# Step sizes of a selective scan: x products one batch ahead, the last batch turned in four banks, the scan's first block beside it

## What is computed

```python
u2 = silu(conv(u) + conv_b)                  # 4 batches x 512 tokens x 512 channels
dbl = u2 @ W_x                               # 48 columns: 16 dt_low, 16 B, 16 C
dt = softplus(dt_low @ W_dt + b_dt)          # step sizes
A = -exp(A_log)
def step(h, inp):                            # 16 states per channel
    dt_t, B_t, C_t, u_t = inp
    dA = exp(dt_t[:, :, None] * A)
    h = dA * h + (dt_t * u_t)[:, :, None] * B_t[:, None, :]
    return h, einsum('bdn,bn->bd', h, C_t)
y = scan(step) + u2 * D
y = y * silu(z)
out = y @ W_out
```

## Time and profile before

| | |
|---|---|
| time before, median of 3 runs | 1596.59 us (1590.95 to 1600.13) |
| the profiled execution | 1599.52 us |
| its span in the profile | 1597.7 us |
| TensorE busy | 1447.3 us (91%) |
| VectorE busy | 1068.1 us (67%) |
| ScalarE busy | 853.1 us (53%) |
| GpSimd busy | 477.2 us (30%) |
| the stage: last z products end, first scan starts | 249.3 us, 333.0 us |

### The profile page before, as it was taken

One profiled execution on the slowest core, in us unless ns is written; L12 is line 12 of the kernel. 1 busy time (PEld: TensorE's weight loads), 2 busy tenths in 40 slices (PEclk: granted clock), 3 DMA queues, 4 the chain that ended last, 5 costly groups with the idle time before them and its releaser, 6 DMA issues.

```text
span 1597.7 us, 20215 instructions
## 1 busy us (share of the span) xinstructions
PE 1447.3 (91%) x7408; PEld 988.6 (62%) x7420; DVE 1068.1 (67%) x1218; ACT 853.1 (53%) x1509; POOL 477.2 (30%) x140
## 2 busy tenths in 40 slices
PE   5898797689899999897999889999989999999997
PEld 3566343278797988743443433333358888888886
DVE  6996495669889898865443457777564565565655
ACT  3433456489989897641432358777733433333332
POOL 0999120059888897600211420000000000000000
PEclk7899999789999999978999989999999999999999
DMA  7110010502233111502012222344000000000000
GB/s 268 40 43 1 1 53 2 199 27 80 106 99 113 67 54 41 175 1 41 20 40 69 81 80 60 102 135 134 1 0 1 1 14 1 1 14 1 14 1 14
DMA packets 36624, 87.61 MB, mean 55 GB/s; under 512 B 8350, under 2 KB 24948, under 8 KB 32948
## 3 DMA queue, kind: packets, MB, share of 16 engines
q1 hardware_dynamic: 36532, 86.39, 16.3%
HBM read 68.10 MB, written 18.21 MB: 54 GB/s over the span
## 4 chain that ended last, share of the span: by engine, by line
PE 55%; DVE 2%; ACT 2%; issue 2%; DVEq 1%; ACTq 0%
PE ps L1424 12%; PE ps L1433 12%; PE ps L1292 4%; PE ps L1365 4%; PE ps L1159 3%; PE ps L1280 2%; PE ps L1185 2%; PE ps L1121 2%; PE ps L991 1%; PE ps L584 1%; ACT arena L1884 1%; PE ps L1334 1%; PE ps L1043 1%; PE ps L1193 1%; PE ps L1171 1%
## 5 line engine op out<-in xcount | busy, mean ns | idle before, releaser
L2567 POOL TENSOR_TENSOR arena<-arena 128x2048 f32<-128x2048 f32 x63 | 287.3, 4579 | 168.4 <-DVE arena L2107 168.2
L2107 DVE TENSOR_TENSOR_SCAN arena<-arena,ps 128x1024 f32<-128x1024 f32 x128 | 284.2, 2272 | 45.0 <-ACT arena L1727 22.4
L1727 ACT ACTIVATE arena<-arena,mam 128x511 f32<-128x511 f32 x256 | 165.9, 708 | 34.4 <-DVE arena L2107 34.4
L1884 ACT ACTIVATE arena<-ps,rho 128x512 f32<-128x512 f32 x256 | 158.9, 688 | 31.3 <-PE ps L1365 29.9
L2339 DVE TENSOR_REDUCE mxs<-ps 128x1 f32<-128x512 f32 x224 | 141.1, 684 | 44.9 <-PE ps L1280 43.0
L979 PE MATMUL ps<-early,arena 128*128 128x128 f32 x768 | 129.7, 277 | 18.2 <-DVE arena L2107 17.8
L1424 PE MATMUL ps<-early,arena 128*128 128x256 f32 x512 | 127.1, 380 | 2.9 <-DVE mam L2506 1.8
L1913 ACT ACTIVATE arena<-arena 128x256 f32<-128x256 f32 x192 | 85.5, 500 | 81.6 <-DVE arena L2510 50.3
L2547 POOL TENSOR_TENSOR arena<-arena 128x4096 f32<-128x4096 f32 x16 | 115.0, 7189 | 43.4 <-DVE arena L2026 43.4
L1715 ACT ACTIVATE arena<-arena,early 128x512 f32<-128x512 f32 x192 | 123.7, 707 | 0.1
L991 PE MATMUL ps<-early,arena 128*128 128x128 f32 x1024 | 121.5, 272 | 0.9 <-POOL arena L2567 0.7
(11 more groups left out here) (351 smaller groups left out, 2486.8 us busy)
## 6 DMA issues: line engine op xcount, KB each, us to landing
arena<-bc_scratch SPq DMA_DIRECT2D x32, 512.0 KB, 3.7
arena<-in_ffn SPq DMA_DIRECT2D x8, 1024.0 KB, 4.8
batch_scratch<-arena SPq DMA_DIRECT2D x2, 3072.0 KB, 9.1
arena<-batch_scratch SPq DMA_DIRECT2D x6, 1024.0 KB, 6.9
arena<-q_scratch SPq DMA_DIRECT2D x96, 64.0 KB, 2.2
arena<-k_scratch SPq DMA_DIRECT2D x96, 64.0 KB, 2.2
arena<-in_dec_w SPq DMA_DIRECT2D x1, 3855.0 KB, 16.1
arena<-in_cond SPq DMA_DIRECT2D x1, 3739.5 KB, 11.5
```

Source lines behind the costliest of these rows:

```text
L1727: last = act.activation(decay[:, (2 * k + h) % 3, i, 1:S], dt[b % 2][:, m, 1:S], ACT.Exp, scale=a_neg[:, m * NS + n:m * NS + n + 1])
L1884: act.activation(pt[:, j % 4, i], ps[:, 3 + (hg + n) % 3, :], ACT.Exp, scale=rho[:, 0:1]).then_inc(s_pt, 1)
L2107: dve.tensor_tensor_scan(half, view(decay[:, (2 * k + h) % 3], [[1, 2 * S]]), view(ps[:, FEED + 2 * h, :], [[1, 2 * S]]), 0.0, ALU.mult, A ...
L2567: pool.tensor_tensor(state[:, k % SLOTS], state[:, k % SLOTS], view(c_rows[:, j % 2, k % G, :], [[0, M], [1, S]]), ALU.mult).then_inc(s_hc, 1)
```

## The change

- TensorE runs the x products of batch i + 1 between the two halves of the step-size products of batch i; those of the second batch behind both halves of the first; those of the first batch between the last two groups of z products, into bank 0. ScalarE's copy into `dbl` moves accordingly: the first between the last two gates, the others behind the Ln of the first half.
- B's transposes stand between the two halves as before, behind the x products.
- `turn_du` and `turned_du` take the banks as an argument. Batches one to three use 6 and 7 twice, as before. The last uses 6 and 7 and then 4 and 5, with no wait between.
- The D products of the first batch stand ahead of the last `turn_du`; the zero that they read is a column of `one` (two wide now) instead of a place in `decay`.
- ScalarE runs `times_b(0)` ahead of the last batch's two copies of du.
- The wait for the second weight load, and for all gates, moves to where it is needed.

```diff
             for b in range(B):
                 for h in range(2):
                     z_products(b, h)
                     if b + 1 < B:
                         u_products(b + 1, (2 * h, 2 * h + 1))
+                    if b == B - 1 and h == 0:
+                        pe.wait_ge(s_up, B * M + 1)
+                        x_products(0, 0)
...
-            for i, b in enumerate(ORDER):
-                pe.wait_ge(s_u2, (b + 2) * M)
-                pe.wait_ge(s_dbl, i + 1)
-                for m in range(M):
-                    last = pe.matmul(ps[0:48, 4, :], w_x[:, m, :], u2[b][:, m, :],
-                                     start=(m == 0), stop=(m == M - 1))
-                last.then_inc(s_x_mm, 1)
-                pe.wait_ge(s_dbl, i + 2)
...
+            for i, b in enumerate(ORDER):
+                pe.wait_ge(s_dbl, i + 2)
+                dt_products(i, 0)
+                if 0 < i < B - 1:
+                    x_products(i + 1, 4)
+                if i:
+                    pe.wait_ge(s_bt, i)
+                else:
+                    pe.wait_ge(s_sz, 2 * B)
+                for t in range(TILES):
+                    last = pe.transpose(ps[:, 5, t * 64:(t + 1) * 64], dbl[0:64, b * S + t * P:b * S + (t + 1) * P],
+                                        ident[0:64, 0:64])
+                last.then_inc(s_bt_mm, 1)
+                dt_products(i, 1)
+                if i == 0:
+                    x_products(1, 4)
+                else:
+                    turn_du(i - 1, (6, 6))
+            pe.wait_ge(s_dt, 2 * B)
+            d_term(0, range(TILES))
+            pe.wait_ge(s_dbl, B + 1)
+            pe.wait_ge(s_bt, B)
+            turn_du(B - 1, (6, 4))
+            pe.wait_ge(s_duT, 2 * B)
+            pe.wait_ge(s_ends, 1)
...
+            def dbl_out(i, bank):
+                act.wait_ge(s_x_mm, i + 1)
+                act.activation(dbl[0:48, tok(ORDER[i])], ps[0:48, bank, :], ACT.Copy).then_inc(s_dbl, 1)
...
+                    if b == B - 1 and h == 0:
+                        act.wait_ge(s_rows, 1)
+                        dbl_out(0, 0)
...
+                    act.activation(soft_l[:, h], soft_e[:, h], ACT.Ln, bias=one[:, 0:1]).then_inc(s_soft, 1)
+                    if h == 0:
+                        if i < B - 1:
+                            dbl_out(i + 1, 4)
+                        act.wait_ge(s_bt_mm, i + 1)
+                        act.activation(bt[:, b], view(ps[:, 5, :], [[64, TILES], [1, NS]], RANK), ACT.Copy).then_inc(s_bt, 1)
+                if i:
+                    turned_du(i - 1, (6, 6))
+            act.wait_ge(s_ends, 1)
+            act.drain()
+            times_b(0)
+            turned_du(B - 1, (6, 4))
+            act.wait_ge(s_dt, 2 * B)
```

More of the change, by code:

```diff
@@ L226, in program @@
         diag = sb("diag", [P, M, P])
-        one = sb("one", [P, 1])
+        one = sb("one", [P, 2])
         at = 0
@@ L910, in _, with x_products @@
             pe.wait_ge(s_lo_out, B // 2 + 1)
+            def x_products(i, bank):
+                b = ORDER[i]
+                pe.wait_ge(s_u2, (b + 2) * M)
+                pe.wait_ge(s_dbl, i + 1)
+                for m in range(M):
+                    last = pe.matmul(ps[0:48, bank, :], w_x[:, m, :], u2[b][:, m, :],
+                                     start=(m == 0), stop=(m == M - 1))
+                last.then_inc(s_x_mm, 1)
             for b in range(B):
@@ L915, in _, with dt_products, turn_du @@
                         u_products(b + 1, (2 * h, 2 * h + 1))
-            pe.wait_ge(s_sz, 2 * B)
-            pe.wait_ge(s_mam, 32)
-            def turn_du(i):
+                    if b == B - 1 and h == 0:
+                        pe.wait_ge(s_up, B * M + 1)
+                        x_products(0, 0)
+            def dt_products(i, h):
+                if i:
+                    pe.wait_ge(s_dt, 2 * i - 1 + h)
+                for m in (2 * h, 2 * h + 1):
+                    last = pe.matmul(ps[:, m, :], wm["w_dt"][:, m * P:(m + 1) * P], dbl[:, tok(ORDER[i])],
+                                     start=True, stop=True)
+                last.then_inc(s_dt_mm, 1)
+            def turn_du(i, banks):
                 pe.wait_ge(s_du, i + 1)
@@ L923, in turn_du @@
                     if i or r:
-                        pe.wait_ge(s_duT, 2 * i + r)
+                        pe.wait_ge(s_duT, 2 * i + (r if banks[0] == banks[1] else 0))
                     for t in (2 * r, 2 * r + 1):
                         for m in range(M):
-                            last = pe.transpose(ps[:, 6 + t % 2, m * P:(m + 1) * P], du[:, m, t * P:(t + 1) * P], ident)
+                            last = pe.transpose(ps[:, banks[r] + t % 2, m * P:(m + 1) * P], du[:, m, t * P:(t + 1) * P],
+                                                ident)
                     last.then_inc(s_duT_mm, 1)
-            for i, b in enumerate(ORDER):
-                pe.wait_ge(s_u2, (b + 2) * M)
-                pe.wait_ge(s_dbl, i + 1)
-                for m in range(M):
-                    last = pe.matmul(ps[0:48, 4, :], w_x[:, m, :], u2[b][:, m, :],
-                                     start=(m == 0), stop=(m == M - 1))
-                last.then_inc(s_x_mm, 1)
-                pe.wait_ge(s_dbl, i + 2)
[L938 to L959, removed]
+            nought = one[:, 1:2].bitcast(BF16)[:, 0:1]
             def d_term(b, tiles):
@@ L1682, in turned_du @@
                     act.wait_ge(s_duT_mm, 2 * i + r + 1)
[L1683 to L1706, removed]
+                    act.activation(duT[ORDER[i]][:, 2 * r:2 * r + 2, :], ps[:, banks[r]:banks[r] + 2, :],
+                                   ACT.Copy).then_inc(s_duT, 1)
             def times_b(k):
@@ L1733, in turned_back @@
                 act.activation(view(zT[b], [[S, 2], [1, S]]), ps[:, 0:2, :], ACT.Copy).then_inc(s_g01, 1)
+            for i, b in enumerate(ORDER):
+                for h in range(2):
+                    act.wait_ge(s_dt_mm, 2 * i + h + 1)
+                    if i:
+                        act.wait_ge(s_dt, 2 * i - 1 + h)
+                    act.activation(soft_e[:, h], ps[:, 2 * h:2 * h + 2, :], ACT.Abs)
+                    act.drain()
+                    act.activation(soft_e[:, h], soft_e[:, h], ACT.Exp, scale=-1.0)
+                    act.drain()
+                    act.activation(soft_l[:, h], soft_e[:, h], ACT.Ln, bias=one[:, 0:1]).then_inc(s_soft, 1)
[4 more added lines that the diff above has]
+                        act.activation(bt[:, b], view(ps[:, 5, :], [[64, TILES], [1, NS]], RANK), ACT.Copy).then_inc(s_bt, 1)
+                if i:
+                    turned_du(i - 1, (6, 6))
+            act.wait_ge(s_ends, 1)
+            act.drain()
+            times_b(0)
+            turned_du(B - 1, (6, 4))
+            act.wait_ge(s_dt, 2 * B)
             for k in range(B * NS):
-                times_b(k)
+                if k:
+                    times_b(k)
                 if k > NS and k % NS == 4:
@@ L2027, in _ @@
                                   kx_row(t, [[0, H], [1, H]], RECIP), ALU.mult).then_inc(s_att, 1)
-            dve.memset(one[:, :], 1.0)
+            dve.memset(one[:, 0:1], 1.0)
+            dve.memset(one[:, 1:2], 0.0)
             dve.wait_ge(s_h0, B * C)
```

5 lines of the change are left out of this document (3 added, 2 removed).

## The result

The changed kernel takes 1585.45 us (median of 7 runs, 1580.31 to 1590.20), the kernel before beside it 1596.59: a ratio of 0.9944, 95% interval 0.9922 to 0.9967. A second comparison, 12 runs of the changed kernel, gave 0.9957, interval 0.9936 to 0.9978. (The quotients of the medians themselves are 0.9930 and 0.9973.) So the change saves 7 to 9 us, about half a per cent. The profiled execution has a span of 1587.3 us, against 1597.7.

What follows compares the result with a forecast made beforehand. A ring of waits among TensorE, ScalarE and VectorE was taken to bound the stage. Ring 3.4 us, 8.7 with the tail, 6.7 arriving: 1599.52 becomes 1592.8, less 2.9 for the median, 1589.9; range 1581 to 1598.5.

Steps and rivals of the forecast that it cites:

- rival 1: Scan start: ScalarE's lost lead doesn't matter, so the whole 8.7 us gain arrives, 1587.9 us; chance 0.15.
- Entry: First batch's x between the last z groups: first Abs 0.45 us earlier, the table load becoming late.
- First lap: Up to the second batch's second Abs: loses 3.0 us because x stands between the two halves of step sizes.
- Second and third lap: Between later batches' second Abs: 15.6 us where it was 17.8, then 13.2 where it was 17.4.
- Tail: Last dt to first scan: D products ahead of the four-bank turns, scan at 324.3, 8.7 us earlier.
- rival 3: Last turns of du: transposes behind matmuls run at 1.2 GHz, gain 4.8 us, 1591.8; chance 0.07.
- What arrives: Scan's first batch: ScalarE, its lead lost, paces; 6.7 of the 8.7 us goes through to the end.
- (2): TensorE keeps 2.4 GHz over the stage's shorter waits: 16.9 us earlier, about 11 if only some restarts are spared; chance 0.20.
- (4): The stage's ring of waits stays at 1.2 GHz, slower than before: 7.5 us later, 1604.1; chance 0.04.
- (5): The ring isn't shortened, x being late as its copy waits on ScalarE's queue: gain about 1 us, 1595.6; chance 0.10.

Runs made afterwards that it cites:

- experiment 1: Changed kernel with both decays of block 0 ahead of ScalarE's last two du copies; first gate 91.0 us behind the last dt instead of 92.9 to 93.7.
- experiment 6: Changed kernel with the first batch's x products behind z, their copy behind the table load; first gate 159.9 us from the last-but-one z group's start, instead of 162.2 to 162.7.
- experiment 7: Changed kernel with third and fourth batches' x products in TensorE's waits; first gate 155.4 us from the last-but-one z group's start, instead of 162.2 to 162.7.
- experiment 5: Changed kernel with TensorE passes nobody reads in its waits; first gate 154.4 us from the last-but-one z group's start, instead of 162.2 to 162.7.
- experiment 2: Changed kernel with the first batch's D products back behind the last turn of du; first gate 94.4 us behind the last dt instead of 92.9 to 93.7.

## Why the prediction held, and where it missed

The forecast was 1589.9 and a gain of 6.7 us; measured were 1585.45 and, at the first gate, 8.5 to 9.4 us by profiles. The gain is a little above the 5 to 8 which the forecast had given itself, and as a number alone rival 1's 8.7 fits better; but rival 1's mechanism is refuted by experiment 1, and the forecast's is borne out step by step, with one term mis-sized. By its own steps:

- **Entry**: forecast 0.45 us, measured 0.15 (14.4 against 14.5 from S). The table load became late, as said; experiment 6 shows it.
- **First lap**: a loss of 3.0 us at the second Abs of batch two forecast, 3.7 measured in the first profile and 2.5 in the two others. x between the halves at 1.2 GHz is what does it: step sizes 3.75 and x 4.71 us (265.22, 268.90). Experiment 7 takes it out and turns the loss into a small gain.
- **Second and third lap**: this is the term that was mis-sized. Forecast 15.6 and 13.2, measured 14.7 and 12.2 to 13.1. I had put turn and first half of step sizes behind the wait at 2.0 + 3.45 us, since each restart was to bring 5 us of 1.2 GHz. In the second lap they take 4.4 in all three profiles, in two ways: in the first the turn is at full clock and the step sizes aren't (280.29 and 281.22, above); in another the turn is slow and the step sizes are so only in part:

```profile
281.19 1.97 PE L944 MATMUL ps<-early,arena 128*128 128x128 f32 x8 [3.49 <-ACT arena L1706]
282.95 2.71 PE L933 MATMUL ps<-arena,mam 128*128 128x512 f32 x4
```

  At full clock the two take 2.7 (experiment 5), so this restart costs 1.7 us. In the kernel before a restart cost 2.8 and 2.4: the turn 1.97 instead of 1.04, and x 5.46 in one lap and 5.12 in the other instead of 3.63. In the third lap turn and step sizes take 4.4 in the first profile and 5.3 in the two others, so there it is cheaper in the first alone. Why a restart costs less in the new ring, though the wait before it is as long (3.49 us in the second lap, 3.42 and 4.55 before), stays open. The last dt came 1.3 to 1.6 us ahead of the forecast.
- **Tail**: D products at 6.6 us forecast; 6.2 to 7 measured. The turns in four banks ran at 2.4 GHz (16 in 1.91 us at 318.13), straight behind matmuls: rival 3 did not come. The Trainium skill (TensorE: Matmul & The Clock Gate, Part 4: PE-mode transpose) says, of transposes in one kernel, that the full clock doesn't engage for transpose mode; these rows show transposes at it. Where transposes come first behind a wait they are slow like other work: in experiment 2 the granted clock was 0.50 over all 16 of them (3.65 us from 315.33) and over the first tile of D products too (1.88 us from 319.20), and 1.00 from 320.9. Last dt to scan 10.6 to 11.4 measured, 11.4 forecast.
- **What arrives**: 2.0 us of the scan's head start were to be lost on ScalarE's missing lead. Measured: 10.3 to 11.1 at the scan, 8.5 to 9.4 at the gate, 1.8 lost. The step was right, and experiment 1 gives the loss back. What it lacked is the second limit, the first scan plus 3.56 us, on which my expectation for experiment 2 failed. In the stretch behind, ScalarE and GpSimd are both full:

```profile
374.00:394.00 20.00, 19.23 (x162) 17.52 (x161) 19.53 (x10) 20.00 (x35) 20.00 (x5) 1.00 0.20 76
```

- **The rivals**: (1), the whole start arrives, falls by experiment 1. (2), the clock holds, did not happen; its price was a gain of 16.9 by the sum, and experiment 5, which makes it happen, has 16.8 at the gate (154.4 against 171.2). (3) and (4) did not show. (5) did not: x is late in the first lap only.
- **In the end**: the median lies 4.5 us below the forecast. 1.8 to 2.3 of it are the stage's, the rest is no more than the scatter of executions, which the second comparison, at 6.9 us of gain, shows from its other side.

## What to carry to other kernels

Work that is taken off a ring of waits is worth the lap that it leaves, and two things decide what that is: whether it stands between two halves for which another engine waits, and what TensorE's clock does in the gap it leaves. Fill the gap with the next products rather than put them behind it. Where a scan or loop starts earlier, ask which engine was ahead of it before: a lead that is lost is paid back from the gain, and the cheapest repair is to hand that engine its first work in the wait just before. And single gains don't add where they live on the same cover.

## What the runs showed of the hardware

TensorE ran at 1.2 GHz in part of every lap with waits of 3.3 to 4.6 us and at 2.4 GHz throughout when the same waits were filled with products that nobody reads; that alone was worth 6 us of 69 in this stage. Where the slow stretch lies behind the same wait differs between executions of the same kernel, and so can its price. The second turn of the first du, behind 3.49 us of idle time each time, took 1.10, 1.76 and 1.97 us in three profiles of the changed kernel, but turn and step sizes together took 4.4 in each. Step sizes and x of the second batch, behind 4.15 us of idle time each time, took 8.3 us in one of the profiles and 7.1 in the two others. A short first instruction behind a wait therefore doesn't show that the restart was free: here it was followed by step sizes of 3.49 us where 1.88 is the time at full clock (experiment 5).
